# Normed rows as fp16 halves, transposed by DMA, in a gated cross-attention and expert kernel

## The chip, the cores and the metric

One core of a Trainium2 chip runs the whole kernel in one launch. The metric is the device time in microseconds, from three runs of the kernel before.

## The reference, cut to what matters

Tokens are 2 x 2048 rows of width 512. Attention goes to 128 context tokens with 16 heads; then come a router with the two best of 8 experts (512 to 256 and back), and a shared expert (512 to 512 and back).

```python
x = x + tanh(g_xattn) * xattn(layernorm(x), ctx, ctx, masks, Wq, bq, Wk, bk, Wv, bv)
n = layernorm(x)
probs = softmax(n @ router)
top, idx = top_k(probs, 2)
coef = sum(one_hot(idx, 8) * top[..., None], axis=2)
routed = sum_e coef[:, e] * ((silu(n @ gate[e]) * (n @ up[e])) @ down[e])
shared = (silu(n @ s_gate) * (n @ s_up)) @ s_down
out = x + tanh(g_ffn) * (routed + shared)
```

## The kernel before, in words

Every large product with weights is done on fp16 halves: a value is scaled, its fp16 rounding is the high half, the fp16 rounding of the rest is the low half, and `split_product` runs three matmuls for each chunk of 128 rows (high x high, high x low, low x high). TensorE needs the left operand transposed, with the 512 features on the partitions.

Three stages follow each other. Each engine has a stream of its own, written by `pipeline(engine, body, total, lag)`: one step of the body handles several tiles at once, each part of it a tile that is `lag` steps behind, so the order of the parts in a body is the engine's order of work. Steps are written out at the ends and are a hardware loop between. `tile(J, v, lag, deep)` gives the tile number, how often its buffer was used, and the buffer.

*First stage* (`body`, 32 tiles of 128 tokens, lags 0 to 8): layernorm, query, scores, softmax, values, x1, the second layernorm (`xn2`, DVE L794), the router and the row lists. At lag 6 PE transposes `xn2` (four f32 128 x 128 blocks, in the helper's line L1028) into bank 1; ACT (L598) and DVE (L854) make the halves `x2t` out of it, PE multiplies by the router at the end of its body. At lag 7 SP stores `xn2` in f32 rows (L370, `normed_rows`) and the transposed halves (L372, `normed_transposed`). POOL subtracts the maxima (L466) and scatters token numbers into the experts' lists (L502); DVE finds maxima (L768); ACT does the exponentials (L575, L605) and the queries (L612). The expert weights are split into halves beside it (L642, L898), in every second tile of the loop.

*Expert stage* (`body2`, 71 slots of 128 rows, each of one expert, lags 0 to 4): SP loads the slot's 128 token numbers (L404; its buffer is guarded by the gather four slots back); POOL gathers these rows of `normed_rows` with an indirect DMA (L518); PE transposes them (four f32 blocks, L1028), ACT (L668) and DVE (L955) make halves; then the product with gate and up, SiLU, a row scale, halves of the hidden rows, their transposes (four f16 blocks), the product with down, a scale (L961) and the store of `expert_rows`. Beside its first steps the shared expert's down weights come in: SP issues the 1 MB load behind step 3 (L419), DVE waits for it in its step 1 and takes its maximum (L1010), POOL reduces that over the partitions in its step 2 (L533), ahead of its fourth gather.

*Third stage* (`body3`, 32 tiles): the shared expert on `normed_transposed`, the gather of each token's two expert rows, the sum and the output.

`hold` waits for the given semaphores and, in the loop, counts a semaphore of its own; `need` waits unless the value is known to be zero or less.

## Time and profile before

| what | value |
|---|---|
| median of 3 runs | 1175.54 us (1173.56 to 1176.14) |
| span of the profiled execution | 1178.0 us |
| its own time beside the span | not listed; the span stands for it |
| mean granted TensorE clock | 0.942 |
| PE busy | 1047.6 us (89%) |
| DVE, ACT, POOL busy | 821.4, 530.6, 442.5 us |

Busy shares of an engine are means over stages. Whether an engine bounds a stage is read from how busy it is within that stage, and from what the others wait for. "Idle before <-releaser" is how long an engine stood still before an instruction and whose completion ended that.

### The profile page before, as it was taken

The numbers are of one execution on the slowest core, as the hardware profiler recorded it, in microseconds if no ns is written. First come the engines' busy times: TensorE is split into PE (matmuls) and PEld (weight loads), VectorE is DVE, ScalarE is ACT, GpSimd is POOL, SyncE is SP. The second block draws the span as 40 slices with busy tenths as digits, with TensorE's granted clock in tenths as the row PEclk, the third lists the DMA queues.
The fourth block names the chain that finished last, engine by engine and source line by source line (L and its number), as shares of the span: only waits on it lengthen the run. The fifth ranks groups of instructions, "written<-read, shape, count | busy, mean of one in ns | idle before, by whom it ended". The sixth has DMA issues, their size and how long they took to land.

```text
span 1178.0 us, 26603 instructions
## 1 busy us (share of the span) xinstructions
PE 1047.6 (89%) x7335; PEld 673.1 (57%) x7336; DVE 821.4 (70%) x2932; ACT 530.6 (45%) x1041; POOL 442.5 (38%) x655
## 2 busy tenths in 40 slices
PE   5499858999999999870599999999999999999997
PEld 3377747777777787760255555555554444444443
DVE  3899856887888888875276666666665566666666
ACT  1266526666666666651244444444443222223232
POOL 1345526676666666643212222121210332222322
PEclk9699978998999899985699999999999999999999
DMA  5564572334333223422333333333342544545443
GB/s 194 216 224 164 129 181 75 92 91 91 91 103 95 88 97 91 108 95 32 98 118 108 121 111 121 111 118 114 117 124 73 161 158 154 173 142 174 150 162 125
DMA packets 76731, 146.96 MB, mean 125 GB/s; under 512 B 20912, under 2 KB 23088, under 8 KB 73872
## 3 DMA queue, kind: packets, MB, share of 16 engines
q1 hardware_dynamic: 46512, 66.01, 21.1%
q10 hardware_dynamic: 17280, 44.83, 10.6%
q0 software_dynamic: 12896, 35.58, 9.8%
q8 instruction: 22, 0.36, 0.2%
q14 instruction: 21, 0.17, 0.1%
HBM read 94.04 MB, written 52.35 MB: 124 GB/s over the span
## 4 chain that ended last, share of the span: by engine, by line
PE 59%; issue 14%; DVE 10%; POOL 8%; ACT 4%; DMA 2%; POOLq 1%; another core or an unknown queue 1%; DVEq 0%; ACTq 0%; SPq 0%
PE bank L1036 14%; PE bank L1037 14%; PE bank L1038 14%; PE bank L1028 8%; PE bank L1071 4%; DVE arena L768 3%; PE bank L1089 3%; POOL arena L466 2%; POOL token_of_row L502 2%; DVE arena L857 1%; ACT arena L612 1%; DMA token_of_row<-arena 1%; DVE peak L871 1%; PE bank L1102 1%; PE bank L1103 1%
## 5 line engine op out<-in xcount | busy, mean ns | idle before, releaser
L1028 PE MATMUL bank<-ident,arena 128*128 128x128 f32 (+1 forms) x1592 | 188.4, 266 | 89.6 <-DMA arena<-normed_rows,arena 30.0
L1036 PE MATMUL bank<-weights,arena 128*128 (+1 forms) x682 | 260.2, 382 | 2.1 <-ACT arena L654 1.9
L1037 PE MATMUL bank<-weights,arena 128*128 (+1 forms) x682 | 260.2, 381 | 0.0
L1038 PE MATMUL bank<-weights,arena 128*128 (+1 forms) x682 | 259.8, 381 | 0.0
L1028 PEld LDWEIGHTS bank<-ident,arena 128*128 128x128 f32 (+1 forms) x1592 | 160.4, 132 | 137.1 <-issue 100.3
L518 POOL DMA_INDIRECT arena<-normed_rows,arena x71 | 67.4, 949 | 241.8 <-PE bank L1028 227.0
L1089 PEld LDWEIGHTS bank<-arena 128*128 128x128 f32 x1024 | 128.6, 195 | 36.2 <-issue 27.7
L1071 PE MATMUL bank<-arena 128*128 128x512 f32 x256 | 140.4, 654 | 8.5 <-DVE arena L768 6.8
L466 POOL TENSOR_TENSOR arena<-arena 128x512 f32<-128x512 f32 x96 | 101.7, 1060 | 85.0 <-DVE arena L768 73.7
L768 DVE CUSTOM_DVE_ANT_0 arena<-bank,arena 128x128 f32<-128x128 f32 x512 | 116.8, 283 | 17.8 <-PE bank L1071 14.5
L1089 PE MATMUL bank<-arena 128*128 128x33 f32 x1024 | 125.7, 273 | 3.8 <-ACT arena L568 3.8
L528 POOL DMA_INDIRECT arena<-expert_rows,arena x64 | 62.7, 979 | 174.0 <-DVE arena L989 156.3
L575 ACT ACTIVATE arena<-arena 128x512 f32<-128x512 f32 x96 | 60.6, 631 | 137.4 <-POOL arena L466 137.2
L1038 PEld LDWEIGHTS bank<-weights,arena 128*128 128x128 f16 x682 | 67.0, 98 | 81.0 <-issue 1.5
L1036 PEld LDWEIGHTS bank<-weights,arena 128*128 128x128 f16 x682 | 66.9, 98 | 72.4 <-issue 4.6
L1037 PEld LDWEIGHTS bank<-weights,arena 128*128 128x128 f16 x682 | 66.9, 98 | 69.9 <-issue 1.3
L961 DVE TENSOR_SCALAR arena<-bank,arena,w_back 128x512 f32<-128x512 f32 x71 | 57.5, 809 | 55.6 <-PE bank L1038 55.5
L1102 PE MATMUL bank<-arena 128*128 128x128 f16 x512 | 91.6, 225 | 1.4 <-DVE arena L798 1.4
L1103 PE MATMUL bank<-arena 128*128 128x128 f16 x512 | 91.6, 225 | 0.0
L1104 PE MATMUL bank<-arena 128*128 128x128 f16 x512 | 91.5, 225 | 0.0
L502 POOL DMA_INDIRECT token_of_row<-arena x64 | 66.7, 1042 | 37.4 <-POOL arena L499 17.2
L663 ACT ACTIVATE arena<-arena 128x256 f16<-128x256 f32 x71 | 36.0, 508 | 92.0 <-DVE arena L973 92.0
(170 smaller groups left out, 1890.5 us busy)
## 6 DMA issues: line engine op xcount, KB each, us to landing
expert_rows<-arena ACTq DMA_DIRECT2D x71, 256.0 KB, 2.1
arena<-in_x SPq DMA_DIRECT2D x64, 256.0 KB, 3.8
weights<-in_w_gu ACTq DMA_DIRECT2D x8, 1024.0 KB, 4.9
x_rows<-arena SPq DMA_DIRECT2D x32, 256.0 KB
normed_rows<-arena SPq DMA_DIRECT2D x32, 256.0 KB, 5.5
normed_transposed<-arena SPq DMA_DIRECT2D x32, 256.0 KB, 2.6
arena<-normed_transposed SPq DMA_DIRECT2D x32, 256.0 KB, 3.2
arena<-x_rows SPq DMA_DIRECT2D x32, 256.0 KB, 3.5
```

Of the source, the lines that this page charges most:

```text
L466: g.tensor_tensor(sc, sc, mx, ALU.subtract).then_inc(shift_done, 1)
L502: g.indirect_dma_start(list_dram, bass.IndirectOffsetOnAxis(ap=row_i[u][:, k:k + 1], axis=0), tok_i[u], None).then_inc(rows_out[u], 16)
L768: last = d.tensor_tensor_reduce(score[u][:, hh * T:(hh + 1) * T], bank[2 + k % 2][:, h * T:(h + 1) * T], mask_bias[u], 1.0, LOWEST, ALU.ad ...
L1028: last = t.transpose(dst[:, c * P:(c + 1) * P], src[:, c * P:(c + 1) * P], (ident16 if src.dtype == F16 else ident)[:, :])
L1036: t.matmul(dst, hi[:, rows], w_hi(c), start=(c == 0), stop=False)
L1037: t.matmul(dst, hi[:, rows], w_lo(c), start=False, stop=False)
L1038: last = t.matmul(dst, lo[:, rows], w_hi(c), start=False, stop=(c == chunks - 1))
L1071: t.matmul(bank[2 + k % 2][:, :], q_t[u][:, k * P:(k + 1) * P], kbd[:, u, k, :], start=True, stop=True).then_inc(s_done, 1)
L1089: last = t.matmul(bank[6 + half][:, at:at + D + 1], probs_t[k % 2][:, h * P:(h + 1) * P], vaug[:, u, k * HG + h, :], start=True, stop=True)
L1102: t.matmul(dst, wq[:, 0, at:at + P], x_hi[:, xs], start=(ci == 0), stop=False)
L1103: t.matmul(dst, wq[:, 0, at:at + P], x_lo[:, xs], start=False, stop=False)
L1104: last = t.matmul(dst, wq[:, 1, at:at + P], x_hi[:, xs], start=False, stop=(ci == EC - 1))
```

## The change

`xn2` is no longer transposed by PE. ACT makes its high half and DVE its low half out of the rows in SBUF, side by side in `xs` (128 x 1024 fp16). SP issues one transposing DMA for it (SBUF to SBUF, into `x2t`, eight 128 x 128 blocks) and stores `xs` as `normed_rows`, so that a row has both halves in the same 2048 bytes. ACT's copy moves from behind its fourth probability copy to behind the first, DVE's from near the end of its body to behind the first maxima; PE waits for the DMA ahead of the router product. The store of `x2t` waits for the transpose a step later.

In the expert stage the gathered rows are already halves. PE's four transposes, ACT's and DVE's copies go. SP, behind the index load of slot s, waits for the gathered rows of slot s-1 and for the product of slot s-5, and issues a transposing DMA into `xgt` (four buffers), which PE reads. POOL's gather of a slot waits for the transpose of the slot four back in place of PE's.

The declarations of semaphores are left out below.

```diff
--- before.py
+++ after.py
@@ -51,7 +51,7 @@
     HALF = NT // B
 
     x1_dram = nc.dram_tensor("x1_rows", [TOK, E], F32).ap()
-    xn_dram = nc.dram_tensor("normed_rows", [TOK, E], F32).ap()
+    xn_dram = nc.dram_tensor("normed_rows", [TOK, 2 * E], F16).ap()
     xt_dram = nc.dram_tensor("normed_transposed", [NT, P, 2 * E], F16).ap()
     list_dram = nc.dram_tensor("token_of_row", [LISTS, 1], I32).ap()
     y_dram = nc.dram_tensor("expert_rows", [SLOTS * P, E], F32).ap()
@@ -126,7 +126,7 @@
         slot_expert = sb("slot_expert", [P, SLOTS], I32)
 
 
-        ARENA = 21 * 1024
+        ARENA = 21 * 1024 + 576
         arena = sb("arena", [P, ARENA])
         top = [0]
 
@@ -150,7 +150,8 @@
         q_t = [carve(E) for _ in range(2)]
         attn = carve(E)
         x1 = [carve(E) for _ in range(2)]
-        xn2 = [carve(E) for _ in range(2)]
+        xn2 = [carve(E)] * 2
+        xs = [carve(E).bitcast(F16) for _ in range(2)]
         x2t = [carve(E).bitcast(F16) for _ in range(2)]
         bv_s = attn
         ctx_s = arena[:, top[0] - 3 * E:top[0] - E].rearrange("p (c n) -> p c n", c=EC)
@@ -181,10 +182,9 @@
         top[0] = 0
         SD = DS // P * E
         swd = carve(SD).bitcast(F16).rearrange("p (a n) -> p a n", a=2)
+        xgt = [carve(E).bitcast(F16) for _ in range(4)]
+        xg = [carve(E).bitcast(F16) for _ in range(4)]
         id_in = [carve(1).bitcast(I32) for _ in range(4)]
-        xg = [carve(E) for _ in range(4)]
-        g_hi = [carve(E // 2).bitcast(F16) for _ in range(2)]
-        g_lo = [carve(E // 2).bitcast(F16) for _ in range(2)]
         g_act = [carve(DX) for _ in range(2)]
         g_h = [carve(DX) for _ in range(2)]
         g_h_hi = [carve(DX // 2).bitcast(F16) for _ in range(2)]
@@ -366,9 +366,7 @@
                     sp.dma_start(x1_dram[bass.ds(j * P + u * S, P), :], x1[u]).then_inc(x1_out[u], 16)
                 n, j, u = tile(J, v, 7)
                 if live(n, NT):
-                    sp.wait_ge(xn2_ready, n + 1)
-                    sp.dma_start(xn_dram[bass.ds(j * P + u * S, P), :], xn2[u]).then_inc(xn2_out[u], 16)
-                    sp.wait_ge(x2t_ready, n + 1)
+                    hold(sp, sp_passed, (x2t_here[u], 16 * (j + 1)))
                     sp.dma_start(xt_dram[bass.ds(n, 1)].rearrange("a p d -> (a p) d"), x2t[u]).then_inc(x2t_out[u], 16)
                 n, j, u = tile(J, v, 0)
                 if live(n, NT):
@@ -381,6 +379,13 @@
                 if live(n, NT):
                     need(sp, x1_ready, n - 1)
                     sp.dma_start(x_res[u], x_tiles[bass.ds(j + u * HALF, 1)].rearrange("a p d -> (a p) d")).then_inc(res_here[u], 16)
+                n, j, u = tile(J, v, 6)
+                if live(n, NT):
+                    hold(sp, sp_passed, (xs_ready, n + 1))
+                    hold(sp, sp_passed, (logits_done, n - 1))
+                    hold(sp, sp_passed, (x2t_out[u], 32 * j))
+                    sp.dma_start_transpose(x2t[u].rearrange("p (c t) -> p c t", t=P), xs[u]).then_inc(x2t_here[u], 16)
+                    sp.dma_start(xn_dram[bass.ds(j * P + u * S, P), :], xs[u]).then_inc(x2t_out[u], 16)
 
             def beside(it):
                 if it == NT + 1:
@@ -390,8 +395,7 @@
             pipeline(sp, body, NT, LAG1, beside=beside, head=HEAD1)
             for u in range(2):
                 sp.wait_ge(x1_out[u], 16 * HALF)
-                sp.wait_ge(xn2_out[u], 16 * HALF)
-                sp.wait_ge(x2t_out[u], 16 * HALF)
+                sp.wait_ge(x2t_out[u], 32 * HALF)
                 sp.wait_ge(rows_out[u], 16 * TOP * HALF)
             sp.wait_ge(plan_ready, 1)
             sp.drain().then_inc(pass1_over, 1)
@@ -402,6 +406,11 @@
                     need(sp, xg_here[u], 16 * j)
                     r = sp.value_load(slot_row[0:1, bass.ds(s, 1)], min_val=0, max_val=LISTS - P)
                     sp.dma_start(id_in[u], list_dram[bass.ds(r, P), :]).then_inc(id_here[u], 16)
+                s, j, u = tile(J, v, 1, 4, SPAN2)
+                if live(s, SLOTS):
+                    hold(sp, sp_passed, (xg_here[u], 16 * (j + 1)))
+                    hold(sp, sp_passed, (gu_done, s - 3))
+                    sp.dma_start_transpose(xgt[u].rearrange("p (c t) -> p c t", t=P), xg[u]).then_inc(xgt_here[u], 16)
 
             def body3(J, v):
                 n, j, u = tile(J, v, 0)
@@ -514,7 +523,7 @@
             def body2(J, v):
                 s, j, u = tile(J, v, 0, 4, SPAN2)
                 if live(s, SLOTS):
-                    hold(pool, pool_passed, (gt_done, s - 3), (id_here[u], 16 * (j + 1)))
+                    hold(pool, pool_passed, (xgt_here[u], 16 * j), (id_here[u], 16 * (j + 1)))
                     g.indirect_dma_start(xg[u], None, xn_dram, bass.IndirectOffsetOnAxis(ap=id_in[u], axis=0)).then_inc(xg_here[u], 16)
 
             def body3(J, v):
@@ -575,6 +584,12 @@
                         a.activation(sc, sc, ACT.Exp).then_inc(exp_done, 1)
 
                 take_probs(0)
+                n, j, u = tile(J, v, 6)
+                if live(n, NT):
+                    act.wait_ge(xn2_ready, n + 1)
+                    need(act, x2t_here[u], 16 * j)
+                    need(act, x2t_out[u], 32 * j)
+                    a.activation(xs[u][:, 0:E], xn2[u], ACT.Copy, scale=X_SCALE).then_inc(xs_hi_ready, 1)
                 take_probs(1)
                 exponent(0)
                 n, j, u = tile(J, v, 7)
@@ -590,12 +605,6 @@
                 exponent(1)
                 take_probs(2)
                 take_probs(3)
-                n, j, u = tile(J, v, 6)
-                if live(n, NT):
-                    act.wait_ge(x2t_done, n + 1)
-                    need(act, logits_done, n - 1)
-                    need(act, x2t_out[u], 16 * j)
-                    a.activation(x2t[u][:, 0:E], bank[1][:, :], ACT.Copy, scale=X_SCALE).then_inc(x2t_hi_ready, 1)
                 exponent(2)
                 n, j, u = tile(J, v, 3)
                 if live(n, NT):
@@ -661,11 +670,6 @@
                     act.wait_ge(g_scale_done, s + 1)
                     need(act, g_ht_done, s - 1)
                     a.activation(g_h_hi[u], g_h[u], ACT.Copy, scale=g_scale[u]).then_inc(g_h_hi_done, 1)
-                s, j, u = tile(J, v, 0, 2, SPAN2)
-                if live(s, SLOTS):
-                    act.wait_ge(gt_done, s + 1)
-                    need(act, gu_done, s - 1)
-                    a.activation(g_hi[u], bank[u][:, :], ACT.Copy, scale=X_SCALE).then_inc(g_hi_ready, 1)
                 s, j, u = tile(J, v, 1, 2, SPAN2)
                 if live(s, SLOTS):
                     act.wait_ge(gu_done, s + 1)
@@ -789,14 +793,17 @@
                 n, j, u = tile(J, v, 6)
                 if live(n, NT):
                     dve.wait_ge(ln2_std, n + 1)
-                    need(dve, x2t_done, n - 1)
-                    need(dve, xn2_out[u], 16 * j)
+                    need(dve, xs_hi_ready, n)
                     d.tensor_scalar(xn2[u], x1[u], mv2[u][:, 0:1], norm2[u][:, 1:2], ALU.subtract, ALU.mult).then_inc(xn2_ready, 1)
                 n, j, u = tile(J, v, 2)
                 if live(n, NT):
                     dve.wait_ge(hi_ready, n + 1)
                     d.scalar_tensor_tensor(x_lo, bank[0][:, :], X_SCALE, x_hi, ALU.mult, ALU.subtract).then_inc(lo_ready, 1)
                 maxima(0)
+                n, j, u = tile(J, v, 6)
+                if live(n, NT):
+                    dve.wait_ge(xs_hi_ready, n + 1)
+                    d.scalar_tensor_tensor(xs[u][:, E:2 * E], xn2[u], X_SCALE, xs[u][:, 0:E], ALU.mult, ALU.subtract).then_inc(xs_ready, 1)
                 if live(n8, NT):
                     dve.wait_ge(rank_done, n8 + 1)
                     if live(n7, NT):
@@ -848,10 +855,6 @@
                     d.tensor_scalar(prob_all[:, bass.ds(n7 * TOP, TOP)], r_top[:, 0:TOP], r_inv, None, ALU.mult)
                     dve.wait_ge(first_done, n7 + 1)
                     d.tensor_tensor(chosen[u7], first[u7], second[u7], ALU.add).then_inc(chosen_done, 1)
-                n, j, u = tile(J, v, 6)
-                if live(n, NT):
-                    dve.wait_ge(x2t_hi_ready, n + 1)
-                    d.scalar_tensor_tensor(x2t[u][:, E:2 * E], bank[1][:, :], X_SCALE, x2t[u][:, 0:E], ALU.mult, ALU.subtract).then_inc(x2t_ready, 1)
                 if live(n0, NT):
                     dve.wait_ge(x_here[u0], 16 * (j0 + 1))
                     d.bn_stats(stats[u0], x_in[u0]).then_inc(ln1_stats, 1)
@@ -948,11 +951,6 @@
                     dve.wait_ge(g_h_hi_done, s + 1)
                     need(dve, g_ht_done, s - 1)
                     d.scalar_tensor_tensor(g_h_lo[u], g_h[u], g_scale[u], g_h_hi[u], ALU.mult, ALU.subtract).then_inc(g_h_lo_done, 1)
-                s, j, u = tile(J, v, 0, 2, SPAN2)
-                if live(s, SLOTS):
-                    dve.wait_ge(g_hi_ready, s + 1)
-                    need(dve, gu_done, s - 1)
-                    d.scalar_tensor_tensor(g_lo[u], bank[u][:, :], X_SCALE, g_hi[u], ALU.mult, ALU.subtract).then_inc(g_lo_ready, 1)
                 s, j, u = tile(J, v, 3, 2, SPAN2)
                 size = g_size[(v - 3) % 4]
                 if live(s, SLOTS):
@@ -1115,19 +1113,15 @@
                 scores(3)
                 turn_probs(2)
                 turn_probs(3)
-                n, j, u = tile(J, v, 6)
-                if live(n, NT):
-                    pe.wait_ge(xn2_ready, n + 1)
-                    need(pe, r_exp_done, n)
-                    need(pe, at_row_done, n - 1)
-                    transposes(bank[1], xn2[u], EC).then_inc(x2t_done, 1)
                 queries((0, 1))
                 queries((2, 3))
                 mix_values(2)
                 mix_values(3)
                 n6, j6, u6 = tile(J, v, 6)
                 if live(n6, NT):
-                    pe.wait_ge(x2t_ready, n6 + 1)
+                    pe.wait_ge(x2t_here[u6], 16 * (j6 + 1))
+                    need(pe, r_exp_done, n6)
+                    need(pe, at_row_done, n6 - 1)
                 n, j, u = tile(J, v, 7)
                 if live(n, NT):
                     pe.wait_ge(chosen_done, n + 1)
@@ -1158,18 +1152,14 @@
                     dst = bank[5][:, :].bitcast(F16)
                     transposes(dst[:, 0:DX], g_h_hi[u], DX // P)
                     transposes(dst[:, DX:2 * DX], g_h_lo[u], DX // P).then_inc(g_ht_done, 1)
-                s, j, u = tile(J, v, 0, 4, SPAN2)
-                if live(s, SLOTS):
-                    pe.wait_ge(xg_here[u], 16 * (j + 1))
-                    need(pe, g_lo_ready, s - 1)
-                    transposes(bank[u % 2], xg[u], EC).then_inc(gt_done, 1)
                 s, j, u = tile(J, v, 1, 2, SPAN2)
+                _, i, x = tile(J, v, 1, 4, SPAN2)
                 if live(s, SLOTS):
                     e = pe.value_load(slot_expert[0:1, bass.ds(s, 1)], min_val=0, max_val=NX - 1)
-                    pe.wait_ge(g_lo_ready, s + 1)
+                    pe.wait_ge(xgt_here[x], 16 * (i + 1))
                     need(pe, g_h_ready, s - 1)
                     w = 2 * DX
-                    split_product(bank[2 + u][:, :], g_hi[u], g_lo[u],
+                    split_product(bank[2 + u][:, :], xgt[x][:, 0:E], xgt[x][:, E:2 * E],
                                   lambda c: gu[:, bass.ds(e * (2 * CH) + c * w, w)],
                                   lambda c: gu[:, bass.ds(e * (2 * CH) + (CH + c * w), w)]).then_inc(gu_done, 1)
                 s, j, u = tile(J, v, 3, 2, SPAN2)
```

## Rows read from the trace of the kernel before

**Rows 1.** The page's first line.

```profile
span 1178.0 us, 26603 instructions
```

**Rows 2.** Windows: busy us of each engine, granted PE clock, DMA share, GB/s.

```profile
184.00:530.00 346.00, 320.20 (x2971) 266.01 (x2968) 283.41 (x1521) 222.35 (x483) 220.84 (x312) 0.94 0.37 95
...
560.00:590.40 30.40, 16.47 (x63) 7.89 (x64) 8.08 (x15) 6.59 (x11) 8.36 (x9) 0.65 0.34 101
...
600.00:880.00 280.00, 279.60 (x1596) 148.01 (x1595) 192.01 (x433) 126.37 (x245) 57.64 (x61) 1.00 0.38 117
...
584.00:586.00 2.00, 2.00 (x7) 1.15 (x8) 0.29 (x1) 0.60 (x1) 0.99 (x2) 0.50 0.63 205
```

**Rows 3.** The gathers' line L518 between 600 and 880 us.

```profile
L518 POOL DMA_INDIRECT arena<-normed_rows,arena x61: 944/944/953, 601.2 to 874.4; - x61
```

**Rows 4.** Line groups, 600 to 880: busy us, mean ns, idle before, releaser.

```profile
L518 POOL DMA_INDIRECT arena<-normed_rows,arena x61 | 57.6, 945 | 220.2 <-PE bank L1028 220.2
...
L955 DVE SCALAR_TENSOR_TENSOR arena<-bank,arena 128x512 f16<-128x512 f32 x61 | 42.0, 689 | 0.0
...
L668 ACT ACTIVATE arena<-bank 128x512 f16<-128x512 f32 x61 | 35.2, 577 | 0.0
```

**Rows 5.** Time line of PE, first stage: start us, us, work.

```profile
438.94 1.47 PE L1028 MATMUL bank<-ident,arena 128*128 128x128 f32 x12
...
440.25 0.22 PE L1102 MATMUL bank<-arena 128*128 128x128 f16 x1
...
459.89 1.50 PE L1028 MATMUL bank<-ident,arena 128*128 128x128 f32 x12 [1.50 <-ACT arena L612]
```

**Rows 6.** Time line, start of the expert stage: SP's queue, POOL, PE.

```profile
559.96 0.35 SPq L404 DMA_DIRECT2D arena<-token_of_row  x1
...
561.05 0.35 SPq L404 DMA_DIRECT2D arena<-token_of_row  x1
...
562.78 1.00 POOL L518 DMA_INDIRECT arena<-normed_rows,arena  x1 [10.54 <-DMA arena<-token_of_row]
...
566.84 1.09 PE L1028 MATMUL bank<-ident,arena 128*128 128x128 f32 x4 [24.38 <-DMA arena<-normed_rows,arena]
```

**Rows 7.** DMA issues: KB, median us to landing (gathers: 591 to 877).

```profile
expert_rows<-arena ACTq DMA_DIRECT2D x71, 256.0 KB, 2.1
...
normed_rows<-arena SPq DMA_DIRECT2D x32, 256.0 KB, 5.5
...
arena<-in_w_down SPq DMA_DIRECT2D x1, 1024.0 KB, 10.1
...
arena<-in_s_down SPq DMA_DIRECT2D x1, 1024.0 KB, 5.8
...
arena<-normed_rows,arena POOLq DMA_INDIRECT x63, 3.4
```

**Rows 8.** Time line, the weight load at the start of the expert stage.

```profile
563.58 0.42 SPq L419 DMA_DIRECT2D arena<-in_s_down  x1
...
577.28 2.27 DVE L1010 TENSOR_REDUCE peak<-arena 128x1 f32<-128x2048 f32 x1
...
580.36 1.19 POOL L518 DMA_INDIRECT arena<-normed_rows,arena  x1 [0.19 <-issue]
...
590.39 0.83 PE L1028 MATMUL bank<-ident,arena 128*128 128x128 f16 x8
```

**Rows 9.** Time line, a first-stage tile without weight split: DVE, POOL, ACT, PE.

```profile
463.60 0.08 DVE L768 DVE_READ_ACCUMULATOR2_ANT arena<- 128x1 f32 x1
...
467.80 1.04 POOL L466 TENSOR_TENSOR arena<-arena 128x512 f32<-128x512 f32 x1 [0.60 <-DVE arena L768]
...
468.87 0.63 ACT L575 ACTIVATE arena<-arena 128x512 f32<-128x512 f32 x1 [0.21 <-POOL arena L466]
...
472.56 1.51 PE L1028 MATMUL bank<-ident,arena 128*128 128x128 f32 x12
```

**Rows 10.** The chain that ended last, 518 to 560 us: the scatter.

```profile
537.26 11.43 DMA token_of_row<-arena
```

More of the change, by code:

```diff
@@ L255, in build @@
             "x1_ready ln2_stats ln2_mv ln2_eps ln2_std xn2_ready")
[L256 to L257 removed]
+        xs_hi_ready, xs_ready, logits_done, logit_max, logit_shift, r_exp_done, r_inv_done, r_top_done = sems(
+            "xs_hi_ready xs_ready logits_done logit_max logit_shift r_exp_done r_inv_done r_top_done")
         r_idx_done, first_done, chosen_done, rank_done, at_row_done, row_f_done, row_ready, tok_ready, seen_done, seen_zero = sems(
```

14 lines of the change are left out of this document (6 added, 8 removed).

## The prediction

> **What bounds the kernel now.** I read the page's first line, then a table by stage, then the time line of one unit of work in each stage, last the DMA issues. The span is 1178.0 us [rows 1]; the stages differ [rows 2]. In the expert stage (600 to 880 us) PE is busy 279.6 of 280 us at full clock. In the first stage (184 to 530) it is busy 320 of 346 with DVE at 283: PE leads there, with gaps. From 560 to 590 nothing is full: a serial start.
>
> The expert stage handles a slot every 4.55 us: its gathers on POOL start from 601.2 to 874.4, 60 periods [rows 3]. ACT's and DVE's copies of the transposed rows (577 and 689 ns each) lie beside PE, and the gathers waited 220 us for PE's transposes: everything but PE runs ahead and then waits for a buffer that PE frees [rows 4].
>
> In the first stage twelve f32 transposes start at 438.94 and the next matmul at 440.25, 0.109 us each [rows 5]. Four of the twelve go: 0.44 us. A slot of the expert stage has four of the same shape among its transposes, so there 0.44 us goes too.
>
> **Expert stage, what it removes.** PE's slot falls from 4.55 to 4.11 us. ACT loses 0.58 and DVE 0.69 us a slot; neither was the bound, so nothing comes of that. Of 71 slots about 65 run in the steady rhythm: at best 65 x 0.44 = 29 us.
>
> **Expert stage, what it adds: a ring on SP.** SP's order of a step becomes: load the slot's row and issue the index load of slot s; wait for the gathered rows of slot s-1; issue the transpose of s-1. Before, SP waited only for a gather four slots back, so the indices ran ahead. Now index load s+1 is queued behind the wait for gather s-1, and gather s+1 can't start without it. Followed round, one trip (index load of s, its gather, its transpose, then index load of s+2) spans two slots: twice the period is at least the sum of
> - index load issued to the gather's start: 2.8 us (559.96 to 562.78 in the first slot [rows 6]);
> - gather's start to its rows landed: 3.4 us [rows 7], and 0.2 for SP to wake (my estimate; PE's first start is 4.06 us after the gather's, with the 1 MB load beside it [rows 6]);
> - from one issue's end to the next index load's start: 0.75 us (561.05 - 559.96 is 1.09, less 0.35 for the issue [rows 6]);
> - X: the time of SP in issuing the transpose, plus what the index load is late because it is queued behind that transfer on the same queue.
>
> So period = (7.15 + X)/2, and PE's 4.11 where that is more. PE stays the bound only for X under 1.07; the slot costs what it does today at X = 1.95. The extra buffers (four xg, four xgt) don't loosen this ring.
>
> No row shows a transposing DMA, so X is bounded by the nearest ones. Below: an ordinary issue on SP takes 0.33 us and delays nobody, X = 0.33 [rows 6]. A loss below nothing is excluded, since SP issues no transpose now. Above: 1 MB loads, four times the bytes, land 5.8 us after their issue on an empty queue and 10.1 us on a busy one [rows 7]; X = 5.8, and as the far end 10.1. Between: a plain store of the same 256 KB lands in 2.1 us alone, but the normed rows' store, issued some 0.6 us behind another 256 KB store on SP's queue, lands in a median of 5.5 [rows 7]; being behind costs about 3 us. The index load is issued 0.75 us behind the transpose. I take X = 2.8, near what being queued behind 256 KB costs. Period 4.98 us, 0.43 over today: +28 us over 65 slots. DMA bandwidth isn't the reason: its share is 0.38 in this stage [rows 2].
>
> What the pages say of the price stands apart from this sum. The Trainium skill (Advanced Engine Details and Errata, X-Bar Transpose) says a transposing DMA is as fast as an ordinary one; by that X would be near 0.33 to 1 and PE the bound. No run here shows it. [...]
>
> **Start of the expert stage.** The shared expert's 1 MB weight load is issued by SP behind step 3, at 563.58 now; DVE waits for it inside its step 1, and POOL's fourth gather waits for DVE's maximum of it until 580.36 (the maximum starts at 577.28, when the load is long there) [rows 8]. In the new order step 3 holds the transpose of slot 2. First rows are there at 566.8 [rows 6]; transpose and next index load put index 2 near 570; its rows land near 576.5; its transpose and then the weights are issued near 579 and land near 584.6. The maximum ends near 587 where it ended at 579.6, and the fourth gather starts 7 us later. Part is hidden, since PE's fourth product stood behind the transposes of 590.39 anyway [rows 8]; I take +5, with +2 for cheap and +8 for dear transposes.
>
> **First stage.** PE loses 0.44 us a tile. ACT's copy (0.58 by its like of the same shape) moves ahead of its second probability copy; DVE's low half (0.69 by its like [rows 4]) moves ahead of the second maxima. Tiles alternate. In the tile with the weight split, PE waits 1.50 us for ACT's L612 [rows 5], behind which ACT worked without a gap since before the copy: the moved copy gives back about 0.5 us there. In the other tile the order is DVE's maxima, POOL's subtraction at 467.80 (idle 0.60 for DVE), ACT's exponent at 468.87 (idle 0.21 for POOL), L605, L612, and PE's next transposes at 472.56, some 0.4 us behind L612 [rows 9]. The low half pushes that chain by 0.7 while PE arrives 0.44 earlier: +0.3. A pair of tiles gains some 0.2 to 0.3 us, 14 pairs: -4 us. Bounds: all of PE's saving, 32 x 0.44 = -14, and +10 if every tile is pushed 0.3. The wait that is new here, PE's for the transpose, has cover: the maxima ahead of the low half end at 463.60, so that it is done near 464.4; PE wants the result near 472, 7.6 us later, more than every X but the largest. At the end of the stage the chain is a scatter of 11.43 us, issued for tile 29, which doesn't need the last tiles' transposes [rows 10]: 0.
>
> **Third stage.** It reads the same bytes; 0.
>
> **Sum.** 1178.0 + 28 + 5 - 4 = 1207. The profiled execution's own time isn't listed beside its span, so the span stands for it; the median of the runs is 2.5 us under it: **1205 us**.
>
> **Rivals.**
> - *Cheap transposes, PE stays the bound* (the other side: faster). Place: SP's ring; price -0.44 a slot; it decides from X under 1.95 and is whole under 1.07. For it: issues of 0.33 us and DMA engines that are mostly idle. Against: the ring needs 7.15 us of the 8.2 that two slots leave. 1178 - 29 + 2 - 4 = 1147, less 2.5: 1145 us. X from 1.07 to 1.95 fills 1145 to 1175. Together 0.29. By the skill's X-Bar rule above this is the case.
> - *Dear transposes, X near 5.8.* Period 6.5, +125, start +8: 1307, less 2.5: 1304 us. For it: 5.5 us for a store queued behind another. Against: moving 256 KB alone takes 2.1. Chance 0.16.
> - *The transpose holds the queue like the slowest 1 MB load, X = 10.1* [rows 7]. Period 8.6, +265; in the first stage 2.5 us a tile beyond the cover, +80; start +15: 1534, less 2.5: some 1530 us. Chance 0.05. The Trainium skill's page on VectorE (VectorE: DVE Perf Modes, The three transpose paths) gives 1309 ns for one 128 x 128; the eight of a slot one after another, an estimate of 10.5 us from that page, would be this case. No row bears on it.
> - *PE's clock falls in the gaps.* In the start, 584 to 586, PE is busy throughout at 0.50 granted (1.2 GHz), after it had been idle [rows 2]. A slot at that level takes twice 4.11, 8.2 us, above my 4.98. Against: my gaps are 0.9 us a slot, and the first stage, with 26 us of gaps up to 1.50 [rows 5], kept 0.94. If it held half of the slots: +105. Chance 0.05.
>
> **How the numbers follow.** Forecast 0.40, the rivals 0.29, 0.16, 0.05, 0.05; the last 0.05 for no difference (X close to 1.95). Range: 1142 (cheap, with more of the first stage's saving) to 1305 (dear). The likeliest's own range, X 2.2 to 4, is 1185 to 1245. About 0.2% is what a measurement tells from no change. Faster 0.29, within it 0.05, slower 0.66.
>
> **What would show it.** Transposes on SP's queue: their issue time and landing give X. Right: in the expert stage PE is busy near 83%, waiting for the transpose about once a slot, gathers start 2.8 us behind their index loads and SP waits for gathers; period near 5. Wrong: gathers wait for PE or for the old buffers, PE at 100%, period 4.1. First stage: the span to 530 within 10 us of before; PE's wait for the transposed tile at zero. Start: fourth gather about 7 us later. The forecast is also wrong if the first stage moves by over 15 us.

## The result, and the profile after

| | before | after |
|---|---|---|
| median of the runs, us | 1175.84 (1173.56 to 1177.84) | 1217.28 (1214.18 to 1218.72) |
| profiled span, us | 1178.0 | 1216.9 |

The ratio is 1.0347, 95% interval [1.0323, 1.0370]: slower, 12 us above the forecast of 1205. The page of after begins with the span and the busy time of each engine:

```profile
span 1216.9 us, 25773 instructions
...
PE 1026.5 (84%) x6923; PEld 643.3 (53%) x6924; DVE 781.1 (64%) x2861; ACT 499.9 (41%) x970; POOL 454.2 (37%) x655
```

Its list of DMA issues has the new ones (32 in the first stage, 71 in the expert stage; median us to landing):

```profile
arena<-arena SPq DMA_TRANSPOSE x103, 3.1
```

By stage, in the columns of [rows 2]; the second stretch is the same 30.4 us from the first index load on:

```profile
184.00:530.00 346.00, 303.99 (x2715) 248.14 (x2714) 271.43 (x1428) 214.15 (x458) 212.89 (x295) 0.93 0.45 106
577.00:607.40 30.40, 13.26 (x44) 5.31 (x45) 5.52 (x11) 4.18 (x7) 5.79 (x6) 0.63 0.45 113
620.00:900.00 280.00, 248.07 (x1270) 118.89 (x1269) 141.10 (x349) 90.75 (x173) 59.37 (x58) 0.99 0.64 162
```

In the expert stage PE is busy 248.1 us of 280 (88.6%) where it was 279.6 [rows 2]. In the first stage it has less to do and still gets through fewer instructions in the same 346 us (2715 against 2971).

Where the 38.9 us of span went, by three marks in the time lines. The first index load of the expert stage starts at 577.01 (before 559.96 [rows 6]): **17.0 us were lost in the first stage**. The fourth gather starts at 601.06, 24.1 us later (before 20.4, [rows 6, 8]): **3.7 at the start**. From there to the end 615.8 us pass, against 597.6: **18.2 in the slots**. All three are in these lines of SP's queue and POOL (start us, us, work):

```profile
577.01 1.46 SPq L408 DMA_DIRECT2D arena<-token_of_row  x2
...
591.41 1.24 SPq L413 DMA_TRANSPOSE arena<-arena  x1
592.70 0.58 SPq L428 DMA_DIRECT2D arena<-in_s_down  x1
...
601.06 1.19 POOL L527 DMA_INDIRECT arena<-normed_rows,arena  x1 [0.19 <-issue]
```

**The ring of the expert stage.** The groups of the gather's line (620 to 900 us) and of the transpose's answer [rows 3, 4]:

```profile
L527 POOL DMA_INDIRECT arena<-normed_rows,arena x58: 947/948/2553, 618.9 to 896.3; - x58
...
L413 SPq DMA_TRANSPOSE arena<-arena x58: 1256/1263/2063, 624.4 to 899.9; - x58
its engine sat idle before it (us, times) until:
who waited for it (us, times):
  PE bank L1034: 31.2, 54
```

57 periods in 277.4 us: 4.87 us a slot, against 4.55. PE waited for the transpose 54 times, and no gather waited for PE any more. One trip around, from the time line:

```profile
700.22 0.36 SPq L408 DMA_DIRECT2D arena<-token_of_row  x1
701.99 1.27 SPq L413 DMA_TRANSPOSE arena<-arena  x1
704.57 0.35 SPq L408 DMA_DIRECT2D arena<-token_of_row  x1
706.84 1.26 SPq L413 DMA_TRANSPOSE arena<-arena  x1
709.44 0.35 SPq L408 DMA_DIRECT2D arena<-token_of_row  x1
...
703.23 0.95 POOL L527 DMA_INDIRECT arena<-normed_rows,arena  x1 [4.01 <-DMA arena<-token_of_row]
```

The index load at 700.22 lets the gather start at 703.23 (3.0 us); its rows let the transpose start at 706.84 (3.6); that holds SP until 708.10 (1.26); the index load after next starts at 709.44 (1.3). Sum 9.2 for two slots; the mean over 57 is 9.7. Over slots 13 to 65 the four parts have means of 3.0, 4.0, 1.3 and 1.4 us, so the trip shown is one with a quick gather.

**The first stage.** What PE waited for between 184 and 540 us (line waited for: us in total, times, longest), in the kernel after:

```profile
PE bank L1130 <- DMA arena<-arena: 25.4, 9, 4.8
PE bank L1069 <- DVE arena L772: 13.5, 23, 2.2
```

L1130 is the first matmul behind PE's wait for the transposed tile; L1069 is the scores' matmul, which needs a bank that DVE's maxima free. The same view of the kernel before:

```profile
PE bank L1028 <- ACT arena L612: 13.3, 11, 1.6
...
PE bank L1071 <- DVE arena L768: 4.0, 3, 2.1
```

### The profile page after: what moved, and what is told of

Its sections match the earlier page's. It is cut to its first block, busy times and chain, and to the rows that moved or that the text cites. A ratio compares the mean times of both kernels' runs of the same rounds, so it can differ in the third digit from the quotient of the medians.

```text
span 1216.9 us, 25773 instructions
## 1 busy us (share of the span) xinstructions
PE 1026.5 (84%) x6923; PEld 643.3 (53%) x6924; DVE 781.1 (64%) x2861; ACT 499.9 (41%) x970; POOL 454.2 (37%) x655
## 4 chain that ended last, share of the span: by engine, by line
PE 30%; issue 21%; DMA 19%; DVE 12%; POOL 7%; SPq 6%; ACT 4%; POOLq 1%; DVEq 0%; another core or an unknown queue 0%; ACTq 0%
DMA arena<-normed_rows,arena 15%; PE bank L1034 7%; PE bank L1036 7%; PE bank L1035 7%; SPq L413 4%; DVE arena L772 4%; PE bank L1026 3%; PE bank L1069 3%; POOL arena L475 2%; ACT arena L621 2%; PE bank L1087 2%; POOL token_of_row L511 1%; DMA arena<-in_x 1%; DVE peak L874 1%; DMA arena<-token_of_row 1%
## 5 line engine op out<-in xcount | busy, mean ns | idle before, releaser
L527 POOL DMA_INDIRECT arena<-normed_rows,arena x71 | 73.6, 1037 | 271.8 <-issue 170.0
L1026 PE MATMUL bank<-ident,arena 128*128 128x128 f32 (+1 forms) x1180 | 142.9, 265 | 34.6 <-DVE arena L757 18.1
L1026 PEld LDWEIGHTS bank<-ident,arena 128*128 128x128 f32 (+1 forms) x1180 | 121.8, 131 | 79.9 <-issue 43.1
L1087 PEld LDWEIGHTS bank<-arena 128*128 128x128 f32 x1024 | 132.2, 199 | 51.6 <-issue 29.9
L1069 PE MATMUL bank<-arena 128*128 128x512 f32 x256 | 140.9, 656 | 17.2 <-DVE arena L772 17.1
L475 POOL TENSOR_TENSOR arena<-arena 128x512 f32<-128x512 f32 x96 | 106.6, 1110 | 109.1 <-DVE arena L772 99.5
L1087 PE MATMUL bank<-arena 128*128 128x33 f32 x1024 | 129.6, 277 | 18.9 <-ACT arena L577 18.7
L1100 PE MATMUL bank<-arena 128*128 128x128 f16 x512 | 89.7, 222 | 1.4 <-DVE arena L801 1.4
L1101 PE MATMUL bank<-arena 128*128 128x128 f16 x512 | 89.7, 222 | 0.0
L1102 PE MATMUL bank<-arena 128*128 128x128 f16 x512 | 89.7, 222 | 0.0
L577 ACT ACTIVATE arena<-bank 128x512 f32<-128x512 f32 x128 | 72.2, 589 | 8.3 <-PE bank L1026 8.3
```

What stands on the lines that cost most here:

```text
L475: g.tensor_tensor(sc, sc, mx, ALU.subtract).then_inc(shift_done, 1)
L1026: last = t.transpose(dst[:, c * P:(c + 1) * P], src[:, c * P:(c + 1) * P], (ident16 if src.dtype == F16 else ident)[:, :])
L1069: t.matmul(bank[2 + k % 2][:, :], q_t[u][:, k * P:(k + 1) * P], kbd[:, u, k, :], start=True, stop=True).then_inc(s_done, 1)
L1087: last = t.matmul(bank[6 + half][:, at:at + D + 1], probs_t[k % 2][:, h * P:(h + 1) * P], vaug[:, u, k * HG + h, :], start=True, stop=True)
L1100: t.matmul(dst, wq[:, 0, at:at + P], x_hi[:, xs], start=(ci == 0), stop=False)
L1101: t.matmul(dst, wq[:, 0, at:at + P], x_lo[:, xs], start=False, stop=False)
```

## The experiments

Each runs beside the kernel before on its own chip, whose median there was 1181.2 us for those named a, 1184.2 for b and 1186.0 for c; so ratios are compared, not times. A single run has no ratio.

Two marks are read from one profile of each kernel: the start of the first index load, and "the 23 steps", the time from PE's router product of tile 4 to that of tile 27 (327.5 us before, 350.7 after). Both marks spread. Kernels with the same first stage as the change give 577.0, 580.2, 582.9 and 591.6 us for the load (after, a1, a2, b4) and 350.7, 356.3, 352.6 and 362.1 us for the steps; the two with a3's order alone give 568.1 and 578.3 us, 340.5 and 344.3 (a3, b2). The kernel before was profiled once, on the first chip. So differences of a few us between such marks show nothing; where the two disagree, the ratio decides.

**a1: index loads ahead of the transposes in the expert stage.**

```diff
-                s, j, u = tile(J, v, 1, 4, SPAN2)   # SP: wait for the rows, transpose
+                s, j, u = tile(J, v, 2, 4, SPAN2)
```

> Against the changed kernel (1217.3 us): in the expert stage SP issues the transpose of slot s-2 behind the index load of slot s, in place of s-1, so two indices are under way during the wait. Ring theory: the ring now spans three slots (9.7 / 3 = 3.2 us), PE is the bound again at 4.1 us a slot; 65 x (4.87 - 4.11) = -49, and 2 to 5 off the start: 1163 to 1170 us. Rival, the DMA engines: with a transpose, a gather and a store in each slot they (0.64 busy over 4.87 us, so 3.1 us) or the one-at-a-time transposes set the pace; the period stays within 0.15 of 4.87 and the time over 1205.

Measured: 1176.26 us, ratio 0.9953 [0.9929, 0.9976]. A slot takes 4.14 us and PE is full again, with the DMA engines now at 0.80 (view of [rows 2]):

```profile
630.00:840.00 210.00, 208.74 (x1095) 101.63 (x1094) 120.18 (x297) 78.53 (x149) 47.41 (x50) 1.00 0.80 189
```

One number of the code takes the ring away, and with it everything that the change lost: 1.0347 to 0.9953. So neither the transposing DMA's bandwidth nor its landing bounded the stage; SP's order did. The ratio fell by 0.0394, which is 46 us of the 1175.84 before, just under the 47 to 54 expected; that the time itself is above 1163 to 1170 is mostly this chip, where the kernel before took 5.4 us more. The first stage kept its loss (first index load at 580.2).

**a2: a plain DMA of the same 256 KB in the place of the transposing one** (the expert stage's operands aren't transposed here).

```diff
-                    sp.dma_start_transpose(xgt[u].rearrange("p (c t) -> p c t", t=P), xg[u])
+                    sp.dma_start(xgt[u], xg[u])
```

> The expert stage's transposing DMA becomes a plain copy of the same 256 KB between the same buffers, with the same waits; its operands are then not transposed. Ring theory: SP's issue falls from 1.26 to 0.33 us and the index load behind it is late by less; two slots cost 9.7 - 0.9 - 0.3 = 8.5, period 4.1 to 4.4, 1165 to 1185 us. Rival, the price lies in the round of waits alone and not in the transpose: period stays at 4.7 or more, over 1205. The first stage is untouched: index load 0 still near 577 us.

Measured: 1183.9 us in one run; a slot takes 4.31 us, SP's issue a median of 0.471 us:

```profile
L413 SPq DMA_DIRECT2D arena<-arena x51: 323/471/472, 632.5 to 845.8; - x51
```

With the ring intact but X smaller by 0.79 of issue and what follows it, two slots take 1.1 us less. That is the ring's X, varied alone.

**a3: in the first stage, transpose and rows' store ahead of the mask and residual loads.** After the change SP issued them behind a wait for POOL's mask (L377 waited 102.9 us, ten times) and behind two loads.

```diff
                     sp.dma_start(x_in[u], ...)            # input tile
+                n, j, u = tile(J, v, 6)                   # moved up from behind the two loads
+                if live(n, NT): ... sp.dma_start_transpose(x2t[u]...); sp.dma_start(xn_dram..., xs[u])
                     ...                                   # mask load (waits for POOL), residual load
```

> First stage only: SP issues the transpose and the normed rows' store of a tile before the mask load and the residual load of the same step, so it isn't held by the wait for POOL's mask (141 us over 15 steps) and isn't queued behind these loads. Order theory: transposes of every second tile start 2 to 3 us earlier, PE's waits for them (25 us in 9 tiles) fall under 5, and the first index load comes at 558 to 563 instead of 577: 1198 to 1205 us. Rival, the scatter: POOL's scatters of token numbers, 4 to 6 us ahead of each slow transpose, make it take 6 to 8 us instead of 3; then the transposes issued nearer behind the scatters land as late as before, and the time stays over 1210.

Measured: 1208.99 us, 1.0237 [1.0199, 1.0274]. The ratio is 0.011 under the change's 1.0347, some 13 us; the first index load moved from 577.0 to 568.1 us, about half of the way back. PE's wait at the router product, 25.4 us in nine waits in the kernel after, is smaller but not gone; the profile names no releaser for it here:

```profile
PE bank L1132 <- issue: 9.0, 5, 4.0
```

SP's order is one part of the first stage's loss; the rest, 8 us by this mark, is something else.

**a4: the change without the two row scatters of each tile** (the lists stay empty, every slot gathers row 0).

```diff
-                    for k in range(TOP):
-                        g.indirect_dma_start(list_dram, ..., tok_i[u], None).then_inc(rows_out[u], 16)
+                    pool.sem_inc(rows_out[u], 16 * TOP)
```

> POOL's scatters of token numbers in the first stage are left out (semaphores counted without them); the lists stay empty, so every slot gathers row 0 and the expert stage is not to be read. Scatter theory: no transpose in the first stage takes more than 4 us to land though SP's order is unchanged, PE's waits for them fall under 8 us, and the steps to the first index load take 10 to 15 us less beside the 10 us of the scatters' own tail. Order theory: transposes behind the mask and residual loads still land 5 to 8 us after their issue and PE's waits stay near 25 us.

**b1: the same edit on the kernel before.**

> The kernel before, with POOL's scatters of token numbers left out of the first stage (the lists stay empty, every slot gathers row 0; the expert stage is not to be read). It is the counterpart of a4_no_scatter, whose first index load came at 535.9 us against 577.0 with scatters, 41 us less. If the scatters cost most by slowing the transposes, the kernel before gains clearly less from leaving them out: its first index load, 560.0, comes at 543 to 552 (the scatters' tail of some 12 us and little else), and the first stage's change without scatters is a gain of 8 or more. Rival: the scatters cost both kernels the same and the loss of 17 us lies elsewhere: 519 to 525.

Measured, one run each: 1229.0 and 1138.8 us. The first index load is at 535.9 in a4 and 514.1 in b1: leaving the scatters out gives 41 us with the change and 46 without. So they are no reason for the loss, which stays at 22 us. Without their disturbance it is visible in every tile: 23 steps take 324.6 us in a4 and 305.2 in b1, and PE waits 25.3 us in 24 waits for the maxima, 4.0 in three in b1. (a4's expert stage is slower still, 5.67 us a slot: its gathers, all of one row, land in 4.5 us and its index loads in 3.2, against 3.8 and 2.2 in the kernel after.) The time line of one such tile in a4:

```profile
336.66 0.69 DVE L804 SCALAR_TENSOR_TENSOR arena<-arena 128x512 f16<-128x512 f32 x1
336.83 1.42 POOL L475 TENSOR_TENSOR arena<-arena 128x512 f32<-128x512 f32 x1 [3.08 <-DVE arena L770]
337.26 0.16 DVE L809 TENSOR_TENSOR arena<-bank,region_at 128x8 f32<-128x8 f32 x1
337.34 0.92 DVE L810 TENSOR_TENSOR seen<-seen,arena 128x8 f16<-128x8 f16 x1
```

The low half (L804) stands where the change put it, and behind it an addition on 128 x 8, whose like is 0.152 us in the kernel before, lasts 0.92: until 338.26, when POOL's subtraction (started 336.83) ends at 338.25. POOL's own 1.42 is 0.38 over its usual 1.04, close to the 0.43 that was left of L804 when POOL started. In the kernel before none of the 23 additions of the steps starts inside POOL's subtraction; pushed back, all 23 do in a4, and 13 in the kernel after, and exactly these last 0.92. The Trainium skill (SBUF — State Buffer, SBUF: two separate sides) has VectorE and GpSimd share a port pair under an exclusive lock, taken too by a VectorE operation with two SBUF inputs; the trace agrees here, down to L809, which reads a bank and isn't held.

**b2: both orders (a1 and a3).**

> Both orders together: the transposes of the expert stage a slot later behind the index loads, those of the first stage ahead of the mask and residual loads. The two gains lie in different stages and should add: against the changed kernel -41 (a1) and -9 to -13 (a3), so 1163 to 1168 us, 0.985 to 0.99 of the kernel before. If the first stage's order only moved DMA traffic, the sum is not reached and it stays at 1172 to 1177.

Measured: 1170.94 us, 0.9884 [0.9826, 0.9943], as expected. Its one profile is of its slowest run (1177.84 us).

**b3: the expert stage alone.** The first stage's operand is turned by PE as before; the halves of the rows are made besides; expert stage as in a1.

```diff
+                    transposes(bank[1], xn2[u], EC).then_inc(x2t_done, 1)          # PE, as before
+                    d.scalar_tensor_tensor(x2t[u][:, E:2 * E], bank[1][:, :], ...)  # DVE, as before
+                    d.scalar_tensor_tensor(xs[u][:, E:2 * E], xn2[u], ...)          # DVE, behind it
```

> The expert stage's part alone, with indices ahead as in a1: the first stage transposes on PE as before for the router and the shared expert, and makes the fp16 halves of the rows beside it (one more copy on ACT behind its second probability copy, one more on DVE beside the other low half). First stage: nothing waits for a transposing DMA, some 0.6 us more of DVE in a tile; first index load at 561 to 570 instead of 580 (a1). Expert stage 4.14 us a slot as in a1. 1155 to 1166 us, the fastest so far. Rival: DVE's chain carries the extra copy in full (32 x 0.6 = 19): first index load past 575, 1172 or more.

Measured: 1179.59 us, 0.9957 [0.9922, 0.9992], a miss. The expert stage is as in a1 (4.14 us), but the first stage still gives its index load at 584.0: one ACT and one DVE operation more per tile cost about as much as the change did (23 steps: 345.1 us against 327.5), though no transposing DMA stood there, nothing was put ahead of the maxima, and no addition was held. Two things differ from the kernel before, not one: `xn2` has one buffer in place of two, as in the kernel after, so DVE waits for the previous tile's readers before it writes the next.

**b4: the first stage alone**; the gathered halves are turned by PE, as f16.

```diff
-                    sp.dma_start_transpose(xgt[u]...)                                     # SP
+                    transposes(bank[u % 2][:, :].bitcast(F16), xg[u], 2 * EC)             # PE
```

> The first stage's part alone: in the expert stage PE transposes the gathered halves (eight f16 blocks, 0.43 us against 0.44 of the four f32), ACT and DVE copy them to SBUF; no transposing DMA there and no ring on SP. Period 4.55 us a slot as before. The first stage's loss stands alone: first index load near 577, 1195 to 1200 us, 1.012 to 1.018 of the kernel before. Were part of the first stage's loss given back later, or part of the loss of 39 us an effect of both parts together, it would lie under 1190.

Measured: 1209.55 us, 1.0210 [1.0148, 1.0272], at or above the upper end; a slot takes 4.57 us, PE full. So the first stage alone costs 2.1%, and the expert stage with its start the other 1.4.

**c4: the kernel before, with one operation of the low half's form added at the low half's new place** (0.69 us; result unused). Nothing of the change is in it.

```diff
                 maxima(0)
+                n, j, u = tile(J, v, 6)
+                if live(n, NT):
+                    d.scalar_tensor_tensor(spare[:, 0:E], x1[u], X_SCALE, x1[u], ALU.mult, ALU.subtract)
```

> The kernel before with one thing added: a VectorE operation on 128x512 of the low half's form (0.7 us, result not used) at the place where the change puts the low half, between the first and the second maxima. Nothing else of the change is there. Push theory: 0.5-0.7 us on each of some 24-32 steps, 12-20 us, ratio 1.010-1.017. Rival (path: only SP's order and the transposing DMA cost): under 3 us, ratio 1.000-1.003.

Measured: 1203.88 us, 1.0156 [1.0123, 1.0190]; first index load at 580.6, 20.6 us late. The group of the addition between 184 and 540 us (min/median/max ns), before and then in c4, and PE's wait in c4:

```profile
L805 DVE TENSOR_TENSOR seen<-seen,arena x27: 148/152/155, 191.8 to 535.9; 128x8 f16<-128x8 f16 x27
```

```profile
L809 DVE TENSOR_TENSOR seen<-seen,arena x23: 150/924/1339, 191.3 to 527.9; 128x8 f16<-128x8 f16 x23
```

```profile
PE bank L1075 <- DVE arena L769: 16.7, 21, 1.8
```

Its 23 steps take 350.4 us, as the change's do (350.7), and the ratio is a loss of 1.6%, where the first stage alone costs 2.1 (b4). But c4 adds an operation, while the change only moves one: DVE is busy 292.1 us of its 23 steps, against 268.6 before and 274.8 after. b3 adds one late in the body and loses 17.6 us over the same steps without any held addition. So c4 shows that an operation at this place brings the wait at the maxima and the held additions; that the place by itself makes the change's loss, and not the added work, it does not show. Nor is the hold bound to the subtraction having begun: in six of c4's tiles the addition starts in the last 0.3 us of a scatter's issue on POOL and lasts 1.2 to 1.3 us, to the end of the subtraction that follows.

**c1: a4 with the low half behind the second maxima.**

```diff
                 maxima(0)
-                ... d.scalar_tensor_tensor(xs[u][:, E:2 * E], xn2[u], ...).then_inc(xs_ready, 1)
                 ...                                       # ranks, logit maximum
                 maxima(1)
+                ... d.scalar_tensor_tensor(xs[u][:, E:2 * E], xn2[u], ...).then_inc(xs_ready, 1)
```

> The changed kernel with the two row scatters of each tile left out (the lists stay empty, so every slot gathers row 0) and VectorE's low half of the normed tile moved from ahead of the second group of maxima to behind it. In the first two batches the changed first stage without scatters took 324.6 us between the scores of tile 4 and tile 27, and the one before 305.2. Theory (push): that 19 us is VectorE's 0.69 us low half, ahead of maxima for which TensorE's scores wait: the stretch falls to 305-312 us, the row of TensorE waiting for maxima falls from 25.3 us to under 8, and the index load of the expert stage starts at 516-524 us instead of 535.9. Rival (path): it is the transposing DMA and its operand: 322-330 us, or more, since the transposing DMA then starts 1.5-2 us later.

Measured: 1229.2 us in one run; index load at 532.4, 23 steps in 320.9 us. Half a miss: PE's wait for the maxima is gone (3.9 us in 2) and the addition is back at 0.153, but 305 to 312 us was not reached. Two successive tiles of c1, then two of b1:

```profile
235.06:247.71 12.65, 12.52 (x125) 10.42 (x125) 12.16 (x60) 8.08 (x19) 8.77 (x12) 1.00 0.35 94
247.71:262.43 14.72, 13.81 (x124) 11.72 (x124) 10.97 (x69) 11.01 (x24) 6.87 (x11) 0.88 0.42 136
```

```profile
230.58:243.54 12.96, 12.85 (x128) 10.77 (x128) 12.42 (x65) 7.67 (x19) 8.75 (x13) 1.00 0.32 104
243.54:256.74 13.20, 12.81 (x128) 10.78 (x128) 10.38 (x64) 11.12 (x24) 6.47 (x12) 1.00 0.28 101
```

At full clock c1's tile is faster than b1's of the same kind: there is PE's saving of transposes, 0.3 of its 0.44 us. But in 8 of 18 tiles the granted clock is 0.88 or 0.89, in b1 in none of 18, and such a tile is 1.5 us longer. Over the 23 steps PE stands idle 15 us where it stood 29 in a4, and is busy 305.8 us where it was 295.8, with as many instructions (granted clock 0.92 against 0.97): most of the idle time won came back as slower work. In one such tile PE stood 0.34 us for ACT, and the twelve transposes behind it took 2.78 us, where they take 1.50 at full clock:

```profile
344.17 2.78 PE L1024 MATMUL bank<-ident,arena 128*128 128x128 f32 x12 [0.34 <-ACT arena L619]
```

**c2: b2 with the low half behind the second maxima; c3: b2 with the four small operations on ranks and logits there instead**, the low half staying early.

> Both orders of SP turned (index loads ahead of transposes in the expert stage, transposes ahead of the mask and residual loads in the first), and the low half behind the second maxima. With both orders alone the ratio was 0.988. Theory (push, cover enough): 10-18 us less, ratio 0.974-0.981. Rival (cover gone): the transposing DMA starts 1.5-2 us later beside the scatters, which cost TensorE up to 4.8 us in a tile; what is won at the maxima is lost at the logits: 0.985-1.0.

> Both orders of SP turned, and the low half where the change put it; instead the four small VectorE operations on ranks and logit maximum (0.5-0.7 us together) go behind the second maxima. VectorE's work ahead of those maxima is then as in the kernel before, and the transposing DMA starts as early as with the change. Push theory: 8-16 us less than both orders alone, ratio 0.975-0.982, and no new wait of TensorE for the transposing DMA. Rival (the router's chain, from ranks to list, sets the stage's end): ScalarE's exponent of the router and the scatters come 1-2 us later in each step, 0.985-0.995.

Measured: c2 1172.33 us, 0.9884 [0.9853, 0.9914]; c3 1166.22 us, 0.9832 [0.9803, 0.9861]. c2 has exactly b2's ratio, and its 23 steps (341.4) lie between a3's and b2's: moving the low half away gained nothing that can be told from the spread. c3 comes near the expected 0.975 to 0.982 without reaching it: 340.3 us for the steps, index load at 567.3, and PE's wait for the maxima 2.6 us in 2. The held additions are not gone: 9 of 23 last 1.3 to 1.5 us, but behind the maxima, where PE doesn't wait for them. c3 has the lowest ratio found, though its interval overlaps that of b2; most of its lead over c2 lies before the router product of tile 4 (180.6 against 186.5 us), which a single profile doesn't explain.

## Why the prediction was right, and where not

The forecast of 1205 us is 12 under the measured 1217, and that nearness is in part luck. Its terms were +28, +5 and -4 us; they measured +18.2, +3.7 and +17.0, so an error of -10 stood against one of +21. By the prediction's own signs the expert stage came out right and the first stage wrong: it was to move by less than 10 us, with PE's wait for the transposed tile at zero, and "over 15 us" was to count against the forecast; it moved by 17.0, with 25.4 us of that wait.

**What bounds the kernel; what the expert stage loses in PE's work.** Right. With the ring gone PE is full at 4.14 us a slot (a1), 0.42 under 4.55, where 0.44 was read off the transposes.

**The ring on SP.** Right in mechanism, and in size by parts that made up for each other: 4.98 forecast, 4.87 measured, gathers 3.0 us behind their index loads, PE busy 88.6% where 83 was said. a1 removes it by order alone, a2 moves it by X alone, and a4's slower landings lengthen it in the same way. The parts were off against one another. X, taken as 2.8 for issue and for queueing behind 256 KB, was an issue of 1.26 us and little behind it: the gap to the next index load is 1.4 us on the mean, and 1.1 with a2's plain copy, so some 0.25 us belongs to X, which is then 1.5. Everything else in the ring, summed to 7.15, measured 8.1 to 8.2, with the plain copy too: gather to transpose took 4.0, not 3.6, the gap 1.1, not 0.75, index load to gather 3.0 to 3.2, not 2.8. That term was mis-sized; with 7.15 and the X of 1.5 the sum would have said 4.3 us a slot, a gain. The term of 28 us measured 18: a period 0.11 us shorter makes 7 of the 10.

The cheap-transpose rival was true of the transfer (3.1 us to landing), and its condition for a gain (X under 1.95) was met; the stage was slower all the same, by the ring's other parts. The two dear ones are refuted for this stage: SP's X was never near 5.8. The Trainium skill (VectorE: DVE Perf Modes, The three transpose paths), whose 1309 ns a block would have made the dearest, isn't borne out as a price per block: eight blocks landed in 3.1 us. The Trainium skill (DMA: Bandwidth & Descriptors, the table of instruction costs) has the sequencer of what it calls previous generations push such a transpose tile by tile; the trace agrees in direction only, with SP held 1.26 us where a plain copy holds it 0.47. The page's figure is for 8,192 tiles, and no price of this shape can be read from it.

**Start of the expert stage.** Right: +3.7 for +5, with the weight load issued behind the transpose of slot 2 as forecast (592.70, right behind 591.41).

**First stage: the step that failed.** -4 was forecast, at worst +10; it was +17.0. Two parts of that step were wrong.
- *The low half pushes the chain by 0.7 while PE arrives 0.44 earlier: +0.3 in one tile of two.* The push was taken as the operation's own time. It was that and 0.77 us more in half of the tiles (16 of 32 additions in the kernel after last 0.92), since the pushed addition fell into POOL's subtraction; and DVE was on PE's path in tiles of both kinds, by the bank that the maxima free, a wait that the view of before shows only three times for 4.0 us. Without scatters this is the whole loss of the steps: a4 takes 19.4 us more than b1 and waits 21.3 more at the maxima. In the kernel after the wait grew by 9.5 us.
- *The wait for the transposed tile has 7.6 us of cover, more than every X but the largest.* The cover was counted from DVE's end of the low half. When SP would come to issue the transpose was not asked: it stood in front of the mask load, and two loads went ahead. PE waited 25.4 us in nine tiles. a3 shows that SP's order makes 9 us of the stage's loss by the first index load, 13 by the ratio.

The two do not add up: c4 has the one, with an operation more, and loses 20.6 us by the mark, a3 is rid of most of the other and still loses 8. Taken out of the changed kernel, the first gives back little: 3.7 us of the 23 steps in c1, nothing clear in c2 and c3. What one wait stops costing the next takes over, or the clock does, as in c1. So the push is shown as the cause of the wait at the maxima, and for the kernels without scatters of the loss; how much of the 17 us it makes with scatters is not shown.

**Third stage.** 0 forecast; it was not measured apart. From the fourth gather to the last it took 325.0 us against 294.0, and from there to the end 290.9 against 303.6: in the kernel before the gathers ran some three slots ahead of PE, so part of what the ring cost them was not on PE's path. Together that is the 18.2 us.

**PE's clock falls in the gaps.** In the expert stage it did not (0.99). In the first stage it was granted 0.95 over the 23 steps before, 0.93 after, 0.90 in c2 and 0.89 in c3. Fewer gaps did not mean more clock: a4, with PE busy 91.7 of 100 us from 300 on, had 1.00 there, and c1, with fewer gaps (95.4), had 0.95. When a gap costs clock, these runs don't settle.

**What stays open.** With both orders and DVE's share ahead of the maxima as it was, the 23 steps are still 13 us longer than before (340.3 against 327.5). Half of it is idle time of PE, 27 us against 21: at the router product it waits 5.6 us for the DMA and 6.0 with no releaser named, a wait of which these steps show none before, while its wait for ACT's L623 is shorter than before (8.4 against 13.3 at L612). The other half is PE being busy longer, 312.8 us against 306.8, although four transposes a step, 10 us in all, are gone; the granted clock is 0.89 against 0.95. Why it is lower is open. ACT's high half, ahead of the second copy of the probabilities, and the single buffer of `xn2` were not changed alone.

## What to carry to other kernels

A transfer issued from a queue that also waits for other work is as late as that queue's slowest wait: before giving a transpose to a DMA, write down what stands ahead of it there and what is queued behind it, and let the loads that feed the next round be issued first. That order was worth 3.9% here, as much as all the transposes taken from PE (103 x 0.44 = 45 us). An operation moved forward on a nearly full engine costs what it pushes, not what it lasts: look at which neighbour engine's work the pushed operations will now run beside. And a wait that is removed is not yet time won: look at the next wait and at the granted clock.

## What the runs showed of the hardware

- A transposing DMA of 128 x 1024 f16 holds SP 1.26 us at its issue, against 0.47 for the plain one of the same bytes (a2), and lands a median of 3.1 us after it in the expert stage of the kernel after (DMA share 0.64), 3.5 in a1 (0.80); in the first stage of the kernel after the median landing is 5.8 and the largest 8.1, without the scatters 3.1 (a4).
- The Trainium skill (Advanced Engine Details and Errata, X-Bar Transpose) calls it as fast as an ordinary DMA. For the transfer the runs come near that (3.1 us, against 2.1 for the 256 KB store of [rows 7]); for the queue that issues it they don't.
- VectorE's addition of two 128 x 8 tiles in SBUF lasts 0.15 us, or 0.92 when it starts 0.3 to 0.5 us into POOL's 128 x 512 subtraction (all 23 of a4's steps, 13 of 23 after). In 15 tiles of c3 and c4, where it starts at the end of a scatter's issue, less than 0.5 us ahead of such a subtraction, it lasts 1.2 to 1.5; one such start in the kernel before lasts 0.15.
- The two scatters a tile, 128 single elements each, cost either kernel 41 to 46 us of its time to the first index load (one profile each); without them the normed rows' store lands in 2.7 us (b1), where it took 5.5 [rows 7].
